# Attention in one interleaved loop: the steps that bring the next batch in stand one to two units later

## The reference

```
h = relu(layernorm(x))
x1 = relu(layernorm((L_norm @ h) @ Wc + bc)) + h
q, k, v = x1 @ Wq, x1 @ Wk, x1 @ Wv            (4 heads each)
scores = q k^T / sqrt(32), masked by the adjacency
o = softmax(scores) @ v                         (512 x 512 per head and batch)
x2 = layernorm(x1 + o @ Wo + bo)
x = x + layernorm(x2 + gelu(x2 @ W1 + b1) @ W2 + b2)
```

## Time and profile before

| what | value |
|---|---|
| median of 3 runs | 1015.18 us (1006.49 to 1015.77) |
| profiled execution, own time | 1019.77 us |
| its span in the profile | 1017.9 us |
| PE busy | 937.3 us (92%) |
| DVE busy | 617.8 us (61%) |
| ACT busy | 535.1 us (53%) |
| POOL busy | 318.9 us (31%) |

### The profile page before, as it was taken

One profiled execution on the slowest core, in us unless ns is written; L12 is line 12 of the kernel. 1 busy time (PEld: TensorE's weight loads), 2 busy tenths in 40 slices (PEclk: granted clock), 3 DMA queues, 4 the chain that ended last, 5 costly groups with the idle time before them and its releaser, 6 DMA issues. The chain is left out here.

```text
span 1017.9 us, 20046 instructions
## 1 busy us (share of the span) xinstructions
PE 937.3 (92%) x7078; PEld 757.7 (74%) x7078; DVE 617.8 (61%) x2003; ACT 535.1 (53%) x1176; POOL 318.9 (31%) x421
## 2 busy tenths in 40 slices
PE   5998999999999999989699999999999999876995
PEld 4556789999999999978466777777777777655774
DVE  3752333333333333524578988888888888864886
ACT  2232322222222233121588888888888888862674
POOL 0001101111111111203135544555555544222786
PEclk8887999999999999989799999999999999995998
DMA  3000000000000000003354444454545554500122
GB/s 91 1 1 10 11 1 12 20 10 10 10 10 10 10 10 10 12 1 102 87 131 116 118 114 116 114 121 110 124 125 125 126 125 126 126 2 1 42 62 63
DMA packets 47218, 61.54 MB, mean 60 GB/s; under 512 B 4377, under 2 KB 22050, under 8 KB 47138
## 3 DMA queue, kind: packets, MB, share of 16 engines
q1 hardware_dynamic: 47138, 60.51, 23.1%
HBM read 39.53 MB, written 20.97 MB: 59 GB/s over the span
## 5 line engine op out<-in xcount | busy, mean ns | idle before, releaser
L1562 ACT ACTIVATE prob<-prob,low 128x512 f32<-128x512 f32 x256 | 184.0, 719 | 51.4 <-DVE low L1614 49.5
L1614 DVE CUSTOM_DVE_ANT_0 prob<-bank,mask 128x512 f32<-128x512 f32 x256 | 171.5, 684 | 28.6 <-PE bank L1440 27.0
L1453 PE MATMUL bank<-ident,prob 128*128 128x128 f32 x1024 | 161.9, 281 | 12.0 <-ACT probT L1551 11.8
L1453 PEld LDWEIGHTS bank<-ident,prob 128*128 128x128 f32 x1024 | 113.8, 141 | 58.1 <-issue 31.7
L1440 PE MATMUL bank<-k_stack,q_stack 128*128 128x512 f32 x256 | 123.8, 485 | 10.2 <-DVE low L1614 5.0
L1551 ACT ACTIVATE probT<-bank 128x512 f32<-128x512 f32 x176 | 102.6, 583 | 2.9 <-PE bank L1453 1.1
L1083 DVE TENSOR_TENSOR T_lo<-bank,T_hi 128x512 fp32r<-128x512 f32 x48 | 33.1, 689 | 111.9 <-ACT T_hi L921 111.9
L921 ACT ACTIVATE T_hi<-bank 128x512 fp32r<-128x512 f32 x48 | 28.4, 592 | 134.7 <-PE bank L831 91.7
L619 POOL TENSOR_SCALAR var_eps<-mv 128x4 f32<-128x4 f32 x16 | 3.6, 226 | 297.7 <-DVE mv L1036 297.7
L927 ACT ACTIVATE Sq<-bank,trace_inv 128x512 fp32r<-128x512 f32 x64 | 44.0, 687 | 92.3 <-PE bank L754 92.3
L1473 PE MATMUL bank<-probT,v 128*32 128x128 f32 x2048 | 82.3, 279 | 3.2 <-ACT probT L1551 1.1
(11 more groups left out here) (241 smaller groups left out, 1948.1 us busy)
## 6 DMA issues: line engine op xcount, KB each, us to landing
k_stack<-bounce_q SPq DMA_DIRECT2D x64, 256.0 KB, 5.2
q_stack<-bounce_k SPq DMA_DIRECT2D x64, 256.0 KB, 7.6
bounce_q<-k_parts SPq DMA_DIRECT2D x16, 512.0 KB, 2.8
bounce_k<-q_parts SPq DMA_DIRECT2D x16, 512.0 KB, 3.1
x_in<-in_x_dram SPq DMA_DIRECT2D x16, 256.0 KB, 2.7
out_dram<-result SPq DMA_DIRECT2D x16, 256.0 KB, 2.2
A<-in_adj_dram SPq DMA_DIRECT2D x4, 256.0 KB, 3.3
W1s<-in_L_gnn_W_dram SPq DMA_DIRECT2D x1, 128.0 KB, 2.3
```

The source lines that it names most:

```text
L1453: last = pe.transpose(psum[2 + u % 2][:, mt * P:(mt + 1) * P], prob[u % RING][:, mt * P:(mt + 1) * P], ident[:, :])
L1562: act.activation(prob[u % RING][:, :], prob[u % RING][:, :], ACT.Exp, bias=low[:, u % TURNED:u % TURNED + 1], scale=-1.0, accum_out=row_su ...
L1614: dve.tensor_tensor_reduce(prob[u % RING][:, :], psum[u % 2][:, :], mask[:, u // HEADS, :], 1.0, 3e38, ALU.add, ALU.min, low[:, u % TURNED ...
```

## The change

Only numbers of the table change. In units: x1's transpose on PE and its copy on ACT go from 2 to 3; k's product and its rounding on ACT from 3 to 5, q's from 4 to 6; the rest of k on DVE from 4 to 6, the rest of q from 5 to 7; the transpose of the inverse sums on PE from 3 to 4 and its copy on ACT from 4 to 5. `residual` stays at unit 1, the value product at 14, the convolution at 6, score 0 of the next batch at 15. SP's program is unchanged, since it waits only for the rests of k and q. No instruction is added or removed. Batch 0 enters in the first layer's stretch and isn't touched; batches 1 to 15 are.

```diff
-AT_X1, AT_X1T, AT_X1T_OUT, AT_K, AT_Q, AT_K_HI, AT_Q_HI, AT_K_LO, AT_Q_LO = 1, 2, 2, 3, 4, 3, 4, 4, 5
+AT_X1, AT_X1T, AT_X1T_OUT, AT_K, AT_Q, AT_K_HI, AT_Q_HI, AT_K_LO, AT_Q_LO = 1, 3, 3, 5, 6, 5, 6, 6, 7
 AT_V, AT_V_OUT = 14, 14
 AT_CONV, AT_CONV_OUT, AT_Z, AT_Z_OUT, AT_Z_MOMENTS, AT_Z_STD = 6, 9, 10, 11, 12, 14
 AT_Y_MOMENTS, AT_H = 9, (11, 12, 13, 15)
-AT_RINV, AT_SPREAD, AT_SPREAD_OUT, AT_O, AT_PROJ, AT_Z2 = 0, 3, 4, 8, 11, 12
+AT_RINV, AT_SPREAD, AT_SPREAD_OUT, AT_O, AT_PROJ, AT_Z2 = 0, 4, 5, 8, 11, 12
```

## The result

| | before | after |
|---|---|---|
| median of 4 runs | 1015.47 us (1006.49 to 1016.42) | 1047.45 us (1041.60 to 1052.56) |
| profiled execution, own time | 1019.77 us | 1046.06 us |
| mean granted clock in it | 0.955 | 0.954 |

The ratio is 1.0333, with a 95% interval of 1.0253 to 1.0414: slower. The two profiled executions lie 26.3 us apart, the medians 32.0 us.

A forecast was written before the change was run, and what follows sets the result against it. Engines nearly full; the stack transfer, 1.8 us slack against a 3.15 us shift, becomes the bound: 13 x 1.35 = 17.5 us, plus 3.1 and 2, say 23 us, so 1015 + 23 = 1038 us; range 1024 to 1050.

The forecast's parts named there:

- that case: The forecast that the stack becomes the bound of every round: 1038 us, range 1025 to 1046, chance 0.76.
- The bound: SP's DRAM round trip of k and q into the stack, awaited by next batch's score 0: 1.8 us slack, batches 2-14.
- The shift of the rest of k: On DVE, the rest of k was to come 3.15 us later, bounds 2.3 and 3.7 us.
- the walk: Following DVE's and ACT's orders from the mask of unit 4 to the rest of k: 661.2 - 658.05 = 3.15 us.
- The sum: Stall at score 0: 1.35 us in each of 13 rounds, 17.5 us, plus 3.1 and 2 at the ends: 23 us.
- the length of the stack's way: From k's write to the landed stack: SP's queue was to keep its shape, the end moving by 3.15 us.
- The wait at x1T: PE's transpose of the inverse sums waits for ACT's copy of x1T: 0.45 us, to stay within some tenths.
- the forecast of PE's path even within 0.3 us a round: PE's path alone, without the stack, was to come out even within 0.3 us a round.
- One sign that I had named: In the changed profile, DVE was to have fewer idle times for ACT before the rest of q.
- The first, no change: Rival: the stack stays hidden behind score 0; with faster reads 1015 to 1020 us; chance 0.14.
- The second, a gain: Rival: PE's waits of 0.45 and 0.57 us vanish, up to 14 us won, 1001 us; chance 0.06.
- The third, the clock: Rival: each stall drops PE to 1.2 GHz for about 5 us, another 17 us, 1055 us; chance 0.04.

## Why the prediction was right

*The number.* The measured 1047.45 us lie inside the range of 1024 to 1050, but 9 us above the 1038 given as likeliest and above that case's own range of 1025 to 1046. The mechanism was the one forecast; its size came out too small.

*The bound.* It put the loss on one transfer whose slack was 1.8 us, and this held in every test: the loss is there with two numbers of DVE's order changed alone, it goes with half of the reads, and it goes with faster reads.

*The shift of the rest of k.* Forecast 3.15 us. Undisturbed rounds show 12.05 - 9.27 = 2.8 us; the mean over the rounds, with those at a lower clock, is about 3.1. That the mean meets the forecast is in part luck: the walk gave 0.3 us too much, and the spells of low clock, which it didn't hold, made that up.

*The sum.* Forecast 1.35 us a round and 23 us in all; measured 1.95 us a round, 32.8 us in the attention and 32 us between the medians. By parts: 17.5 us forecast for the thirteen rounds and 25.3 measured, 2 and 4.4 ahead of them, 3.1 and 3.1 behind them; the last agrees by luck, since it holds a fall of the clock. The term that was too small is the length of the stack's way, which I took as unchanged. From k's write to score 0 I reckoned 26.4 + 1.35 - 12.4 = 15.3 us; it was 28.4 - 12.4 = 16.0. Part of it is seen: k's write lands late in some rounds. Line L403 in the rounds of batches 6 and 8:

```profile
L403 SPq DMA_DIRECT2D bounce_q<-k_parts x1: 376/376/376, 640.9 to 640.9; - x1
DMA to landing us min/median/max: 4.9/4.9/4.9
```

```profile
L403 SPq DMA_DIRECT2D bounce_q<-k_parts x1: 377/377/377, 697.9 to 697.9; - x1
DMA to landing us min/median/max: 2.8/2.8/2.8
```

The DMA queues in the 2.4 us after each of these writes: in the first stretch a fetch of instructions runs on one of the 16 engines too, in the second none.

```profile
q1 hardware_dynamic: 255, 0.49, 52.5%
q8 instruction: 1, 0.02, 2.5%
```

```profile
q1 hardware_dynamic: 272, 0.52, 57.4%
```

In seven of the 14 rounds from batch 2 to 15 the trace has a fetch of this queue that begins within 2.8 us of k's write, and in these seven the write landed after 4.1 to 5.1 us; in the other seven after 2.7 to 2.9 us. From k's write to score 0 the seven late rounds took 16.5 us on the mean, the others 15.6, so late writes are some 0.4 of the 0.7 us that my reckoning lacked; the rest is open. This is a coincidence in time, not an experiment: no run moved a fetch. In the kernel before, only one such fetch began there (batch 7, landing after 3.4 us), and the slack took it up; batch 5's write landed after 3.6 us with none. Without slack each delay counts.

*The waits of PE.* The wait at x1T was forecast to stay. As a wait for ACT it went, a few tenths of a stop at the same transpose are left, and the mask of unit 4 took over as what PE waits for there. That changed no sum, as the pair with halved reads shows: the forecast of PE's path even within 0.3 us a round was right (26.4 us a round in either order). One sign that I had named failed: DVE's idle time for ACT before the rest of q didn't get less, it went from 9.0 to 12.2 us, in 15 waits each.

*The rivals.* The first, no change, needed reads of 435 GB/s; reads alone went at 213 to 219 (the 235 of the earlier trace rows includes the end of a write), and the slack was what the landings said. The second, a gain, showed only where the stack was made shorter and the rests alone were moved, and then as 0.3 us a round, not 1.0. The third, the clock, came true in part. I had given it 0.04 for every round; it fell in some. Two windows of equal place after score 0, of batches 6 and 7 of the changed kernel:

```profile
659.00:662.00 3.00, 3.00 (x24) 2.04 (x23) 2.74 (x7) 2.10 (x6) 1.94 (x3) 0.50 0.00 0
687.50:690.50 3.00, 2.38 (x28) 1.61 (x27) 2.99 (x8) 2.09 (x6) 1.87 (x3) 1.00 0.00 0
```

After the wait of 2.34 us PE ran at 1.2 GHz for a while, after the one of 1.65 us it stayed at 2.4. From score 0 to the next write of k the round of batch 6 took 670.16 - 657.23 = 12.9 us, 0.9 more than the 12.05 of the other. The trace has six such falls at a wait for the stack, at score 0 of batches 1, 3, 5, 6, 11 and 15; if each costs 0.9 us, an estimate from that one pair, they cost some 5 us in all. Before, it has none between 501.5 and 910 us. The two fastest runs of the changed kernel have a mean granted clock of 0.954, the two slowest, 1048.84 and 1052.56 us, one of 0.947; but this mean takes in the first layer and the MLP, and doesn't tell where the clock fell.

## What to carry to other kernels

Before moving a producer, take its consumer's start minus the landing of the transfer between them, in several rounds: the move is free up to that slack and costs nearly one for one above it, plus every delay that the slack had swallowed. Count the slack on each engine that the moved result passes, POOL too; the later z2 cost 3%, by its waits through a queue that I hadn't looked at. And when a transfer becomes the bound, look at its rate before its start: where the reads wrote was worth 30 us here, in a single index.

## What the runs showed of the hardware

- Reads into 32 neighbouring partitions moved 213 and 219 GB/s with the DMA engines 1.06 and 1.07 busy; the same reads into every fourth partition 292 GB/s at 0.89. The Trainium skill ("SBUF — State Buffer", Door 1: The DMA port swizzle) says that DMA bandwidth depends on how many of the 16 ports the partitions reach. By its table 32 neighbouring partitions reach 8 of them and every fourth partition reaches all 16; half of its 435 GB/s would be an estimated 218, which agrees with the 213 and 219 here. The 292 of the spread rows is below its ceiling, so something else limits there, which no run here separates.
- A fetch of instructions on one DMA engine went with a 512 KB write that landed 1.3 to 2.3 us later, in seven rounds of seven of the changed kernel's trace; the one in the kernel before went with 0.6 us. That the fetch is the cause isn't shown, nor how a single busy engine would hold the write up that long.
- PE's clock fell to 1.2 GHz after waits for the stack of 2.04, 2.34, 2.46, 2.53, 3.00 and 5.35 us and stayed at 2.4 GHz after five of 0.9 to 1.8 us, but also after three of 2.12, 2.13 and 2.52 us; the length of the wait alone doesn't decide it. The Trainium skill ("TensorE: Matmul & The Clock Gate", HAM oscillation) describes kernels that lose the clock in each turn while they wait for a DMA; here it was six times in fifteen.
- Two profiled executions differed in a part with the same instructions: the stretch ahead of the attention took 490.3 us at a mean granted clock of 0.95, PE busy 461.5 us, in one, and 484.8 us at 0.96, PE busy 454.5 us, in the other. The spread from the fastest to the slowest of four runs is much the same for both kernels, 10 and 11 us.
